# Low-rank and router product of tiles 1 to 3 as three rounded products of split operands

## The chip, the cores and the metric

The kernel runs on one core of one Trainium2 chip. The metric is the device time of one execution in microseconds (us), the median of three runs.

## What is computed

The input `x` holds 64 sequences of 32 tokens with 512 features. Two blocks are applied one after the other, each added to its input. Cut to what matters, the reference is:

```python
# block 0
base   = einsum('btd,od->bto', x, W)                  # W: 512 x 512
logits = einsum('btd,ed->bte', x, Wr) + 5.0 * one_hot(language)   # 8 experts
gates  = softmax over the two largest logits, 0 elsewhere
h      = einsum('btd,erd->bter', x, A)                # 8 experts x rank 16 = 128
x      = x + base + 2.0 * einsum('bter,bte,eor->bto', h, gates, B)
# block 1: an adapter of rank 16 per sequence, out of 64
x      = x + einsum('bnr,bor->bno', einsum('bni,bri->bnr', x, B1[id]), A1[id])
```

The two products in question here are `h` (128 columns) and the router's logits (8 columns). Both multiply `x`, so the kernel takes them as one product with 136 columns.

## The kernel before

The 2048 tokens are cut into four tiles (`NB` = 4) of `TB` = 512 tokens. Features lie on the 128 partitions in `K` = 4 blocks: `xs[:, t, k]` is block k of tile t, a 128 x 512 operand. Everything stays in SBUF. The code is written out by hand for each engine, with semaphores between the engines; each engine runs its list in order, so the order of the calls in the code is the order of the work.

**Operands.** A 32-bit operand can be used in two ways. A plain 32-bit operand (F32) goes into one `matmul` call, which the trace shows as two LDWEIGHTS and two MATMUL records. An operand of type float32r (F32R) has been rounded; a call with such operands shows one record of each. To keep the precision, the kernel splits an operand into a rounded part and a rounded rest (`x_hi` and `x_lo`, `w_hi` and `w_lo`, and so on) and takes three products: hi with hi, hi with lo, lo with hi. ScalarE makes the hi part (`round_hi`, L328), VectorE or GpSimd the rest (`split_lo`, L431; L309 on GpSimd for `x_lo` of tiles 1 to 3). `x_hi` and `x_lo` have two slots each, taken in turn by tile.

**TensorE's list per tile.** (`t` is the tile; names as in the code.)

- `base(t, c)`, L613, for output block c of four: 4 calls each on L631 (`w_hi` x `x_hi`), L637 (`w_lo` x `x_hi`) and L643 (`w_hi` x `x_lo`), all with 512 moving columns and accumulating in PSUM bank `main[c]`.
- `aw_first()` for tile 0 and `aw_tiles(u)` for tiles 1 to 3 (L675, L685): the product with 136 columns, in plain 32-bit form. The stationary operand is a 128 x 128 piece of `xs` (128 tokens), the moving one is `aws[:, k]`, 128 x 136. That is 4 token pieces x 4 blocks k = 16 calls (L673) per tile, into the two banks `aw_ps`. The last one signals `aw_done`.
- `gt_transposes(u)`, L696: four transposes of the gated `h`.
- `lora(t, c)`, L646: three products (L657 to L659) that add the low-rank output into `main[c]`.
- `down_part` (L725) and `up` (L749; `up_last`, L762 to L766, for the last tile): the two products of block 1.

The order is at L770 to L817. `aw_tiles(1)` stands between `lora(0, 0)` and `lora(0, 1)`; `aw_tiles(2)` and `aw_tiles(3)` stand behind the last `base` of the tile before and ahead of its `lora(t + 1, 3)`.

**The others.** VectorE waits on `aw_done`, forms the logits, their two largest and the gate (`top_two`, `pick`, `gate_h`), writes `gated`, and adds results to `xs` (L479 for block 0, L528 for block 1). ScalarE rounds `b0`, then takes the exponential of tile 0's gap (`exp_gap(0)`), then rounds `x` of tile 1 (L394 to L398). SyncE issues the loads and stores.

Of the kernel before, what the change touches and what calls it, by code (L numbers as in the profile page):

```python
# [39 lines left out]
P = 128  # L40
F32 = mybir.dt.float32
F32R = mybir.dt.float32r
# [11 lines left out]
def two_block_kernel(nc, x, adapter_id, adapter_list, language_id, w, aw, b0, a1, b1, out, *, tokens_per_batch,  # L54
# [22 lines left out]
    with ExitStack() as ctx:  # L77
        def sb(name, shape, dt=F32):
            return ctx.enter_context(nc.sbuf_tensor(name, shape, dt))
# [4 lines left out]
        def sem(name):  # L84
            return ctx.enter_context(nc.semaphore(name))
# [4 lines left out]
        ws = sb("ws", [P, K, K, P])  # L90
        w_hi, w_lo = sb("w_hi", [P, K, K, P], F32R), sb("w_lo", [P, K, K, P], F32R)
        aws = sb("aws", [P, K, AWN])
        b0s = sb("b0s", [P, D])
        b0_hi, b0_lo = sb("b0_hi", [P, D], F32R), sb("b0_lo", [P, D], F32R)
        rows = sb("rows", [P, SLOTS, D])
# [68 lines left out]
        exp_ready = sem("exp_ready")  # L164

        zeros_ready, w0_hi_ready, w0_lo_ready = sem("zeros_ready"), sem("w0_hi_ready"), sem("w0_lo_ready")
        b0_lo_ready = sem("b0_lo_ready")
        x0_lo_ready, x1_ready = sem("x0_lo_ready"), sem("x1_ready")
        gt_lo_ready = sem("gt_lo_ready")
        down_ready, down_lo_ready = sem("down_ready"), sem("down_lo_ready")  # L170
# [149 lines left out]
        @block.scalar  # L320
        def _(act):
            act.dma_start(aws[:, 0], aw[:, 0]).then_inc(aw_loaded[0], 16)
            act.dma_start(aws[:, 1:], aw[:, 1:]).then_inc(aw_loaded[1], 16)

            act.wait_ge(zeros_ready, 1)
            nc.scalar.activation(table_warm[:], zeros[:, 0:1], ACT.Exp)

            def round_hi(dst, src, ready):  # L328
                nc.scalar.activation(dst, src, ACT.Copy).then_inc(ready, 1)  # L329

            def w_half(c):
                act.wait_ge(w_loaded[c], 16)
                round_hi(w_hi[:, c], ws[:, c], w_hi_ready)

            def x_half(t, c):
                if t == 0:
                    act.wait_ge(x0_loaded[c], 16)
                elif c == 0:
                    act.wait_ge(x_loaded[t], 16)
                    if t >= 2:  # L340
                        act.wait_ge(base_done, (t - 1) * K)
                round_hi(x_hi[:, t % 2, c], xs[:, t, c], x_hi_ready)

            def a1_half(g):
                act.wait_ge(rows_loaded[g], 16)
                if g >= SLOTS:
                    act.wait_ge(up_done, PARTS * (g // GPB - 1))
                s = g % SLOTS
                if packed(g):
                    if g >= GPB:  # L350
                        act.wait_ge(a1_lo_ready, g - GPB + 1)
                    round_hi(a1_hi[:, g % GPB], rows[:, s], a1_hi_ready)
                else:
                    round_hi(a1_ops[:, s, 0], rows[:, s], a1_hi_ready)

            def pack_a1(g):

                act.wait_ge(a1_lo_ready, g + 1)
                s = g % SLOTS
                for h, own in enumerate(halves):  # L360
                    nc.scalar.activation(a1_ops[own, s, h], a1_hi[own, g % GPB], ACT.Copy)  # L361
                    last = nc.scalar.activation(a1_ops[halves[1 - h], s, h], a1_rest[own, g % GPB], ACT.Copy)  # L362
                last.then_inc(a1_packed, 1)

            def exp_gap(u):
                act.wait_ge(gap_ready, u + 1)
                nc.scalar.activation(gap_exp[:], gap[:], ACT.Exp).then_inc(exp_ready, 1)

            def gt_half(u):
                act.wait_ge(gt_done, u + 1)  # L370
                if u >= 1:
                    act.wait_ge(lora_done, u * K)
                round_hi(gt_hi[:], side[1][:], gt_hi_ready)

            def down_half(g):
                act.wait_ge(down_ready, g + 1)
                if g >= SLOTS:
                    act.wait_ge(up_done, PARTS * (g // GPB - 1))
                s = g % SLOTS
                if packed(g):  # L380

                    for to in (0, 1):
                        for h, own in enumerate(halves):
                            last = nc.scalar.activation(down_ops[halves[h ^ to], s, h, 0:GT // 2],  # L384
                                                        down[own, g % GPB, 0:GT // 2], ACT.Copy)
                        last.then_inc(down_hi_ready, 1)
                else:
                    round_hi(down_ops[:, s, 0], down[:, g % GPB], down_hi_ready)

            for c in range(K):  # L390
                x_half(0, c)
            for c in range(1, K):
                w_half(c)
            act.wait_ge(b0_loaded, 16)  # L394
            round_hi(b0_hi[:], b0s[:], b0_hi_ready)
            exp_gap(0)
            for c in range(K):
                x_half(1, c)  # L398
            gt_half(0)
            for t in range(NB - 1):  # L400
                if t == 0:
                    for g in range(GPB):
                        a1_half(g)
                    for g in range(GPB):
                        pack_a1(g)
                exp_gap(t + 1)
                for g in range(t * GPB, (t + 1) * GPB):
                    down_half(g)
                gt_half(t + 1)
                for g in range((t + 1) * GPB, (t + 2) * GPB):  # L410
                    a1_half(g)
                if t + 2 < NB:
                    for c in range(K):
                        x_half(t + 2, c)
                    for g in range((t + 1) * GPB, (t + 2) * GPB):
                        pack_a1(g)
            for g in range((NB - 1) * GPB, NG):
                down_half(g)
# [3 lines left out]
        def _(dve):  # L422
# [31 lines left out]
            def gate_h(u):  # L454

                dve.wait_ge(exp_ready, u + 1)
                then_wait(nc.vector.tensor_scalar(denom[:], gap_exp[:], 1.0, None, ALU.add))
                then_wait(nc.vector.reciprocal(inv[:], denom[:]))
                nc.vector.tensor_scalar(weight[:, :, 0], inv[:], SCALING0, None, ALU.mult)
                then_wait(nc.vector.scalar_tensor_tensor(weight[:, :, 1], gap_exp[:], SCALING0, inv[:],  # L460
                                                         ALU.mult, ALU.mult))

                then_wait(nc.vector.tensor_tensor(
                    picked_w[:], picked[:], weight[:].unsqueeze(3).broadcast_to([P, TILES, 2, experts]), ALU.mult))
                then_wait(nc.vector.tensor_tensor(gate[:], picked_w[:, :, 0], picked_w[:, :, 1], ALU.add))
                if u >= 1:
                    dve.wait_ge(gt_done, u)

                for j, h in h_parts(u):
                    last = nc.vector.tensor_tensor(  # L470
                        gated[:, j].rearrange("p j (e r) -> p j e r", e=experts),
                        h[:, :, 0:H].rearrange("p j (e r) -> p j e r", e=experts),
                        gate[:, j].unsqueeze(3).broadcast_to([P, j.stop - j.start, experts, rank]), ALU.mult)
                    if j.stop in (TILES // 2, TILES):
                        last.then_inc(gated_ready, 1)
# [96 lines left out]
            top_two(0)  # L572
            pick()
            gate_h(0)
            gt_rest(0)
            dve.wait_ge(const_ready, 4)
            then_wait(nc.vector.tensor_tensor(own_in_half[:], own_batch[:, 0:BPG // 2], own_batch[:, BPG // 2:],
# [34 lines left out]
        def _(pe):  # L612
# [54 lines left out]
            def lora_last(s):  # L667
                lora_products(K - 1, last_x1_banks[s][:, 0:GT], slice(s * GT, (s + 1) * GT))

            def aw_product(u, j, k):  # L670

                h = [h[:, j - js.start] for js, h in h_parts(u) if js.start <= j < js.stop][0]
                return nc.tensor.matmul(h, xs[:, u, k, j * P:(j + 1) * P], aws[:, k], start=(k == 0), stop=(k == K - 1))  # L673

            def aw_first():  # L675

                for k in range(K):
                    if k <= 1:
                        pe.wait_ge(aw_loaded[k], 16)
                    pe.wait_ge(x0_loaded[k], 16)  # L680
                    for j in range(TILES):
                        last = aw_product(0, j, k)
                last.then_inc(aw_done, 1)

            def aw_tiles(u):  # L685
                pe.wait_ge(x_loaded[u], 16)

                pe.wait_ge(gated_ready, u * 2)
                if u >= 2:
                    pe.wait_ge(x2_ready, (u - 1) * PARTS)  # L690
                for j in range(TILES):
                    for k in range(K):
                        last = aw_product(u, j, k)
                last.then_inc(aw_done, 1)

            def gt_transposes(u):  # L696
# [157 lines left out]
```

## Time and profile before

| what | value |
| --- | --- |
| median of 3 runs | 107.45 us |
| lowest and highest run | 106.88 and 107.86 us |
| profiled execution, span from first to last instruction | 104.8 us |
| mean granted TensorE clock over the span | 0.961 |
| TensorE busy (MATMUL records) | 93.5 us, 89% |
| TensorE weight loads | 78.2 us, 75% |
| VectorE, ScalarE, GpSimd busy | 68.0, 43.7, 39.0 us |

The profile is of one execution. It gives the span, from the first to the last instruction on the core; a run's time also holds what lies before and after, so the median lies 2.65 us above the span and the lowest run 2.1 us. In the profile, PE is TensorE's matmul side and PEld its weight loads; DVE is VectorE, ACT ScalarE, POOL GpSimd, SP SyncE. In names such as `aw_ps<-aws,xs` the output comes first, then the moving operand, then the stationary one; buffer numbers are left out (`b_hi` is `b0_hi`, `a_ops` is `a1_ops`). Both float32r and plain matmuls are printed as f32. A record's duration includes the time in the pipeline, so durations of neighbours overlap; the pace is read from start to start.

### The profile page before, as it was taken

The page shows a single profiled execution, that of the slowest core. Times are in us where ns is not written, and L with a number is a line of the kernel's source. Part 1 is how long each engine was busy: PE and PEld are TensorE (multiplying, and loading weights), DVE is VectorE, ACT ScalarE, POOL GpSimd, SP SyncE. Part 2 cuts the span into 40 slices and gives each one's busy share as a digit, 9 for nine tenths or more (in the row PEclk, how much of TensorE's full clock was granted, in tenths as well). Part 3 has the DMA queues.
Part 4 walks back from the last instruction along what each step waited for, and adds up shares of the span by engine and source line. Part 5 has one row for each costly group of instructions (what it writes and reads, how often), then busy time and mean ns, then how long its engine had stood idle before and what let it go on. Part 6 is the DMA issues. An engine that isn't in the chain of part 4 may idle for free.

```text
span 104.8 us, 2166 instructions
## 1 busy us (share of the span) xinstructions
PE 93.5 (89%) x733; PEld 78.2 (75%) x733; DVE 68.0 (65%) x220; ACT 43.7 (42%) x88; POOL 39.0 (37%) x42
## 2 busy tenths in 40 slices
PE   5999995009999999999999999999999999999970
PEld 2597882008799788988898888888988888898860
DVE  1269989994421997498604983988029839891890
ACT  3472604405693069802970489009803840000300
POOL 4002986996920000699900004998000072000000
PEclk9999999965599999999999999999999999999997
DMA  2999807426993693222569200222600002314046
GB/s 36 356 348 291 362 19 181 131 62 113 422 276 95 126 356 72 59 55 58 145 154 324 104 0 0 100 100 47 260 0 0 3 0 69 137 52 149 6 168 232
DMA packets 14989, 14.33 MB, mean 137 GB/s; under 512 B 10114, under 2 KB 11394, under 8 KB 14594
## 3 DMA queue, kind: packets, MB, share of 16 engines
q1 hardware_dynamic: 14050, 11.82, 35.1%
q0 software_dynamic: 640, 2.10, 7.2%
q10 hardware_dynamic: 288, 0.28, 1.1%
q8 instruction: 6, 0.10, 0.4%
q14 instruction: 5, 0.04, 0.1%
HBM read 9.99 MB, written 4.19 MB: 135 GB/s over the span
## 4 chain that ended last, share of the span: by engine, by line
PE 87%; issue 7%; DVE 3%; DVEq 0%
PE main L631 15%; PE main L637 14%; PE main L643 14%; PE aw_ps L673 12%; PE side L725 5%; PE main L658 3%; PE main L657 3%; PE main L659 3%; PE aw_ps L749 3%; PE main L772 3%; PE side L673 2%; DVE xs L520 2%; PE side L705 2%; PE main L749 1%; PE side L749 1%
## 5 line engine op out<-in xcount | busy, mean ns | idle before, releaser
L309 POOL TENSOR_TENSOR x_lo<-xs,x_hi 128x512 fp32r<-128x512 f32 x12 | 15.0, 1284 | 25.7 <-ACT x_hi L329 25.7
L631 PE MATMUL main<-x_hi,w_hi 128*128 128x512 f32 (+1 forms) x64 | 18.6, 414 | 0.0
L637 PE MATMUL main<-x_hi,w_lo 128*128 128x512 f32 (+1 forms) x64 | 17.7, 400 | 0.0
L643 PE MATMUL main<-x_lo,w_hi 128*128 128x512 f32 (+1 forms) x64 | 17.0, 387 | 0.0
L637 PEld LDWEIGHTS main<-x_hi,w_lo 128*128 128x128 f32 x64 | 12.4, 197 | 2.8
L673 PE MATMUL aw_ps<-aws,xs 128*128 128x136 f32 x112 | 14.1, 279 | 0.0
L643 PEld LDWEIGHTS main<-x_lo,w_hi 128*128 128x128 f32 x64 | 12.1, 192 | 2.6
L673 PEld LDWEIGHTS aw_ps<-aws,xs 128*128 128x128 f32 x112 | 13.7, 190 | 0.2
L631 PEld LDWEIGHTS main<-x_hi,w_hi 128*128 128x128 f32 x64 | 11.8, 197 | 2.5 <-DVE w_hi L543 0.2
L361 ACT ACTIVATE a_ops<-a_hi 64x512 fp32r<-64x512 f32 x12 | 7.6, 630 | 10.7 <-POOL a_rest L293 10.6
L479 DVE TENSOR_TENSOR xs<-main,xs 128x512 f32<-128x512 f32 x15 | 9.9, 683 | 2.8 <-PE main L659 2.8
L384 ACT ACTIVATE down_ops<-down 64x128 fp32r<-64x128 f32 x24 | 7.4, 309 | 6.3 <-DVE down L494 5.9
L329 ACT ACTIVATE x_hi<-xs 128x512 fp32r<-128x512 f32 x16 | 9.0, 619 | 1.7 <-DMA xs<-x_t 1.7
L528 DVE TENSOR_TENSOR xs<-aw_ps,xs 128x256 f32<-128x256 f32 x24 | 9.2, 415 | 0.1
L277 POOL DMA_INDIRECT rows<-a_t,row_at x8 | 8.7, 1087 | 1.5 <-issue 1.1
L438 DVE TENSOR_TENSOR logits<-aw_ps,bias 128x16 f32<-128x16 f32 (+1 forms) x8 | 1.0, 164 | 12.6 <-PE aw_ps L673 12.6
L705 PE MATMUL side<-ident,gated 128*128 128x128 f32 x16 | 2.9, 312 | 6.6 <-issue 6.6
L293 POOL TENSOR_TENSOR a_rest<-rows,a_hi 128x512 f32<-128x512 f32 x6 | 7.7, 1292 | 0.6 <-ACT a_hi L329 0.6
L528 DVE TENSOR_TENSOR xs<-main,xs 128x256 f32<-128x256 f32 x12 | 4.5, 419 | 5.2 <-PE main L749 5.1
L705 PEld LDWEIGHTS side<-ident,gated 128*128 128x128 f32 x16 | 2.1, 156 | 7.5 <-issue 7.0
L362 ACT ACTIVATE a_ops<-a_rest 64x512 fp32r<-64x512 f32 x12 | 7.6, 630 | 0.1
L293 POOL TENSOR_TENSOR a_ops<-rows,a_ops 128x512 fp32r<-128x512 f32 x2 | 2.5, 1292 | 11.6 <-ACT a_ops L329 11.6
(111 smaller groups left out, 145.8 us busy)
## 6 DMA issues: line engine op xcount, KB each, us to landing
out_t<-xs SPq DMA_DIRECT2D x16, 256.0 KB, 2.3
xs<-x_t SPq DMA_DIRECT2D x3, 1024.0 KB, 6.4
b1s<-b_t SPq DMA_DIRECT2D x64, 32.0 KB, 2.0
xs<-x_t SPq DMA_DIRECT2D x4, 256.0 KB, 4.2
ws<-w_t SPq DMA_DIRECT2D x4, 256.0 KB, 5.6
b0s<-b_t SPq DMA_DIRECT2D x1, 256.0 KB, 5.6
aws<-aw_t ACTq DMA_DIRECT2D x1, 204.0 KB, 4.0
rows<-a_t,row_at POOLq DMA_INDIRECT x8, 4.0
```

The source lines that it names most:

```text
L277: nc.gpsimd.indirect_dma_start(rows[:, g % SLOTS], None, a1, bass.IndirectOffsetOnAxis(ap=row_at[:, g:g + 1], axis=0)).then_inc(rows_loade ...
L293: nc.gpsimd.tensor_tensor(lo, rows[:, s], hi.bitcast(F32), ALU.subtract).then_inc(a1_lo_ready, 1)
L309: nc.gpsimd.tensor_tensor(x_lo[:, t % 2, c], xs[:, t, c], x_hi[:, t % 2, c].bitcast(F32), ALU.subtract).then_inc(x_lo_ready, 1)
L329: nc.scalar.activation(dst, src, ACT.Copy).then_inc(ready, 1)
L361: nc.scalar.activation(a1_ops[own, s, h], a1_hi[own, g % GPB], ACT.Copy)
L362: last = nc.scalar.activation(a1_ops[halves[1 - h], s, h], a1_rest[own, g % GPB], ACT.Copy)
L479: nc.vector.tensor_tensor(xs[:, t, c], main[c][:], xs[:, t, c], ALU.add).then_inc(x1_ready, 1)
L528: return nc.vector.tensor_tensor(to, up_banks[i][:].rearrange("p (h q n) -> p h q n", h=2, q=2)[:, :, part], to, ALU.add)
L631: nc.tensor.matmul(out_ap, w_hi[:, c, k], x_hi[:, s, k, n], start=(k == 0), stop=False)
L637: nc.tensor.matmul(out_ap, w_lo[:, c, k], x_hi[:, s, k, n], start=False, stop=False)
L643: last = nc.tensor.matmul(out_ap, w_hi[:, c, k], x_lo[:, s, k, n], start=False, stop=False)
L673: return nc.tensor.matmul(h, xs[:, u, k, j * P:(j + 1) * P], aws[:, k], start=(k == 0), stop=(k == K - 1))
```

## The change

Tiles 1 to 3 take the product with 136 columns as three products of split operands; tile 0 stays as it is. `aw_tiles` issues 48 calls per tile in place of 16, with the pieces of `x_hi` and `x_lo` that `base` uses as the stationary operand and `aw_hi` or `aw_lo` as the moving one. Two new tensors and two semaphores hold the split of `aws`. ScalarE makes `aw_hi` between `b0_hi` and `exp_gap(0)`; VectorE makes `aw_lo` between `gate_h(0)` and `gt_rest(0)`. `aw_tiles` now waits for `x_hi` and `x_lo` of its tile where it waited for the tile's load.

```diff
+        aw_hi, aw_lo = sb("aw_hi", [P, K, AWN], F32R), sb("aw_lo", [P, K, AWN], F32R)
...
             round_hi(b0_hi[:], b0s[:], b0_hi_ready)
+            act.wait_ge(aw_loaded[0], 16)
+            act.wait_ge(aw_loaded[1], 16)
+            round_hi(aw_hi[:], aws[:], aw_hi_ready)
             exp_gap(0)
...
             gate_h(0)
+            dve.wait_ge(aw_hi_ready, 1)
+            split_lo(aw_lo[:], aws[:], aw_hi[:], aw_lo_ready)
             gt_rest(0)
...
             def aw_tiles(u):
-                pe.wait_ge(x_loaded[u], 16)
+                s = u % 2
+                pe.wait_ge(x_hi_ready, (u + 1) * K)
+                pe.wait_ge(x_lo_ready, u * K)
+                if u == 1:
+                    pe.wait_ge(aw_hi_ready, 1)
+                    pe.wait_ge(aw_lo_ready, 1)
 
                 pe.wait_ge(gated_ready, u * 2)
                 if u >= 2:
                     pe.wait_ge(x2_ready, (u - 1) * PARTS)
                 for j in range(TILES):
+                    h, n = h_tile(u, j), slice(j * P, (j + 1) * P)
                     for k in range(K):
-                        last = aw_product(u, j, k)
+                        nc.tensor.matmul(h, x_hi[:, s, k, n], aw_hi[:, k], start=(k == 0), stop=False)
+                        nc.tensor.matmul(h, x_hi[:, s, k, n], aw_lo[:, k], start=False, stop=False)
+                        last = nc.tensor.matmul(h, x_lo[:, s, k, n], aw_hi[:, k], start=False, stop=(k == K - 1))
                 last.then_inc(aw_done, 1)
```

On TensorE, at the place of tile 1's product between `lora(0, 0)` and `lora(0, 1)`, the kernel before has this (a row is a line, an operation, output<-moving,stationary, the output's shape and a count):

```order
23 L657 MATMUL main<-gt_hi,b_hi 128x512
24 L658 MATMUL main<-gt_hi,b_lo 128x512
25 L659 MATMUL main<-gt_lo,b_hi 128x512
26 L673 MATMUL aw_ps<-aws,xs 128x136 x16
27 L657 MATMUL main<-gt_hi,b_hi 128x512
```

and the changed kernel has this (its lines are numbered a few higher; L663 to L665 are the products of `lora`). The three rows 26 to 28 come 16 times in a row, up to row 73:

```order
23 L663 MATMUL main<-gt_hi,b_hi 128x512
24 L664 MATMUL main<-gt_hi,b_lo 128x512
25 L665 MATMUL main<-gt_lo,b_hi 128x512
26 L704 MATMUL aw_ps<-aw_hi,x_hi 128x136
27 L705 MATMUL aw_ps<-aw_lo,x_hi 128x136
28 L706 MATMUL aw_ps<-aw_hi,x_lo 128x136
```

Sixteen calls have become 48 at the same place, and two of each three neighbours have the same stationary piece of `x_hi`. The other two tiles read alike.

On ScalarE, ahead of tile 0's exponential, the changed kernel has one row more (8):

```order
6 L330 ACTIVATE w_hi<-ws 128x512 x3
7 L330 ACTIVATE b_hi<-b0s 128x512
8 L330 ACTIVATE aw_hi<-aws 128x544
9 L368 ACTIVATE gap_exp<-gap 128x4
10 L330 ACTIVATE x_hi<-xs 128x512 x4
```

On VectorE, behind tile 0's gating, the changed kernel has one row more (31):

```order
30 L474 TENSOR_TENSOR gated<-aw_ps,gate 128x128 x2
31 L436 TENSOR_TENSOR aw_lo<-aws,aw_hi 128x544
32 L436 TENSOR_TENSOR gt_lo<-side,gt_hi 128x512
33 L583 TENSOR_TENSOR own_in_half<-own_batch 128x4
34 L483 TENSOR_TENSOR xs<-main,xs 128x512
```

Nothing else has moved on these two engines; the lists of GpSimd and SyncE are as before.

## Rows read from the trace of the kernel before

**Rows 1.** The page: span, busy time, and slices of TensorE and its clock.

```profile
span 104.8 us, 2166 instructions
...
PE 93.5 (89%) x733; PEld 78.2 (75%) x733; DVE 68.0 (65%) x220; ACT 43.7 (42%) x88; POOL 39.0 (37%) x42
...
PE   5999995009999999999999999999999999999970
...
PEclk9999999965599999999999999999999999999997
```

**Rows 2.** Who waited for whom on TensorE: us in total, times, longest.

```profile
PE side L705 <- issue: 6.6, 1, 6.6
PE main L772 <- DVE zeros L537: 1.3, 1, 1.3
```

**Rows 3.** The chain that ended last, in order: start us, us, what.

```profile
8.07 0.46 PE aw_ps L673 x4
8.54 0.04 issue
8.57 1.20 PE main L631 x4
...
17.05 6.56 issue
23.61 1.12 PE side L705 x4
24.73 1.71 PE main L631 x4
...
29.91 3.71 PE aw_ps L673 x32
...
39.94 0.44 PE side L705 x4
40.37 0.94 PE main L631 x4
...
52.66 3.71 PE aw_ps L673 x32
...
74.04 3.71 PE aw_ps L673 x32
...
93.17 0.48 PE main L637 x4
```

**Rows 4.** Timeline of TensorE, 96.85 to 97.45 us: matmul records of three float32r products.

```profile
96.86 0.39 PE L657 MATMUL aw_ps<-gt_hi,b_hi 128*128 128x256 f32 x1
97.09 0.28 PE L658 MATMUL aw_ps<-gt_hi,b_lo 128*128 128x256 f32 x1
97.21 0.28 PE L659 MATMUL aw_ps<-gt_lo,b_hi 128*128 128x256 f32 x1
```

**Rows 5.** The same timeline, weight loads.

```profile
96.86 0.19 PEld L657 LDWEIGHTS aw_ps<-gt_hi,b_hi 128*128 128x128 f32 x1
96.97 0.19 PEld L658 LDWEIGHTS aw_ps<-gt_hi,b_lo 128*128 128x128 f32 x1
```

**Rows 6.** Timelines of ScalarE and VectorE around the two new instructions.

```profile
12.27 0.61 ACT L329 ACTIVATE b_hi<-b0s 128x512 fp32r<-128x512 f32 x1
17.26 0.20 ACT L367 ACTIVATE gap_exp<-gap 128x4 f32<-128x4 f32 x1 [4.38 <-DVE gap L443]
...
23.48 0.48 DVE L470 TENSOR_TENSOR gated<-aw_ps,gate 128x128 f32<-128x128 f32 x2
25.40 0.69 DVE L432 TENSOR_TENSOR gt_lo<-side,gt_hi 128x512 fp32r<-128x512 f32 x1 [1.44 <-ACT gt_hi L329]
...
30.01 0.69 DVE L479 TENSOR_TENSOR xs<-main,xs 128x512 f32<-128x512 f32 x1 [2.75 <-PE main L659]
```

**Rows 7.** Timeline of GpSimd: the rests of x for tiles 1, 2 and 3.

```profile
18.07 4.92 POOL L309 TENSOR_TENSOR x_lo<-xs,x_hi 128x512 fp32r<-128x512 f32 x4 [0.92 <-ACT x_hi L329]
...
42.78 5.06 POOL L309 TENSOR_TENSOR x_lo<-xs,x_hi 128x512 fp32r<-128x512 f32 x4 [13.19 <-ACT x_hi L329]
...
64.20 5.06 POOL L309 TENSOR_TENSOR x_lo<-xs,x_hi 128x512 fp32r<-128x512 f32 x4 [11.55 <-ACT x_hi L329]
```

More of the change, by code:

```diff
@@ L166, in two_block_kernel @@
         zeros_ready, w0_hi_ready, w0_lo_ready = sem("zeros_ready"), sem("w0_hi_ready"), sem("w0_lo_ready")
-        b0_lo_ready = sem("b0_lo_ready")
+        b0_lo_ready, aw_hi_ready, aw_lo_ready = sem("b0_lo_ready"), sem("aw_hi_ready"), sem("aw_lo_ready")
         x0_lo_ready, x1_ready = sem("x0_lo_ready"), sem("x1_ready")
@@ L668, in lora_last, with h_tile @@
                 lora_products(K - 1, last_x1_banks[s][:, 0:GT], slice(s * GT, (s + 1) * GT))
-            def aw_product(u, j, k):
-                h = [h[:, j - js.start] for js, h in h_parts(u) if js.start <= j < js.stop][0]
-                return nc.tensor.matmul(h, xs[:, u, k, j * P:(j + 1) * P], aws[:, k], start=(k == 0), stop=(k == K - 1))
+            def h_tile(u, j):
+                return [h[:, j - js.start] for js, h in h_parts(u) if js.start <= j < js.stop][0]
             def aw_first():
@@ L681, in aw_first @@
                     for j in range(TILES):
-                        last = aw_product(0, j, k)
+                        last = nc.tensor.matmul(h_tile(0, j), xs[:, 0, k, j * P:(j + 1) * P], aws[:, k],
+                                                start=(k == 0), stop=(k == K - 1))
                 last.then_inc(aw_done, 1)
             def aw_tiles(u):
-                pe.wait_ge(x_loaded[u], 16)
+                s = u % 2
[4 more added lines that the diff above has]
+                    pe.wait_ge(aw_lo_ready, 1)
                 pe.wait_ge(gated_ready, u * 2)
```

## The prediction

> **What bounds the kernel now.** I read the page first. TensorE is busy for 93.5 of 104.8 us, and its line of slices stands at 9 from the tenth slice to the thirty-eighth of forty [rows 1]. The next question is whether it ever waits. The view of waits on TensorE names two waits in the whole span: 1.3 us ahead of the very first matmul and 6.6 us ahead of the transposes of tile 0 [rows 2]. The chain of work that ended last puts the second one at 17.05 to 23.61 us [rows 3]; from there TensorE's list runs through without a wait. So a microsecond more or less in TensorE's list after 23.6 us is a microsecond more or less in the time, unless the change makes some other engine late. The product with 136 columns of tiles 1 to 3 lies in this part: three stretches of 3.71 us, at 29.91, 52.66 and 74.04 us [rows 3], 11.1 us together.
>
> **What is removed.** Each stretch is 16 plain calls, shown as 32 pairs of a weight load and a matmul. 3.71 us by 32 is 0.116 us from one pair to the next, or 0.232 us a call. The clock is at 9 tenths or more in all slices of that part [rows 1], which is the 2.4 GHz level. 0.116 us at 2.4 GHz is 278 cycles, and twice 136 columns is 272: each record of the plain form streams its 136 columns twice and nothing else is seen. A plain call thus costs four passes of 136 columns.
>
> **What is added on TensorE.** 48 calls of the rounded form. A rounded call shows one pair of records. With 256 columns it takes 0.12 us (0.48 us for 4 [rows 3]); 256 columns at 2.4 GHz are 0.107 us, so it is one pass. One pass of 136 columns is 0.057 us, and 48 of them would be 2.7 us, which would be 1.0 us less per tile. That is what the change looks like on paper. But the stream is not the only thing in a pair.
>
> The other thing is the weight load: each call brings its own 128 x 128 stationary operand. As a rule it is hidden behind the stream of the call before. Its true length shows only where TensorE comes out of a gap. At 96.86 us it does. The load for L657 starts at 96.86 and that for L658 at 96.97, 0.11 us later [rows 5]. The first matmul record lasts 0.39 us where its like last 0.28 [rows 4], so 0.11 us passed before it could begin. Both say that a load of 128 columns in the rounded form takes 0.11 us. The second load starts when the first matmul can begin, so one load at a time goes on ahead of the running matmul. In the plain form with 136 columns the load (0.11) hides exactly under two passes (0.116); with 256 columns in the rounded form it hides under one pass. With 136 columns in the rounded form the pass is 0.057 us and no longer covers it: the load sets the pace.
>
> No row shows a rounded call with fewer than 256 columns, so its price is bounded. From below by the load alone, which is printed as 0.11: at least 0.105 us. From above by the rounded call with 256 columns, since fewer columns can't take longer in the same form: 0.12 us [rows 3, 4]. The end nearest to the case is the load, because the stream is now well under it; I take 0.112 us. Then 48 x 0.112 = 5.38 us replace 3.71 us: +1.67 us per tile, and for three tiles +5.0 us. The ends: 48 x 0.105 = 5.04 us gives +4.0 us in all; 48 x 0.12 = 5.76 us gives +6.2 us.
>
> **The two new instructions.** `aw_hi` is a rounding of 544 columns; one of 512 takes 0.61 us [rows 6], so about 0.65 us. ScalarE stands idle for 4.38 us after `b_hi` until tile 0's gap comes from VectorE at 17.26 us [rows 6]; the two loads of `aws` that it waits for have landed long before, since TensorE is through with tile 0's product, which uses them, at 8.57 us [rows 3]. Cost nothing; without that idle time it would delay the exponential, and with it the transposes that TensorE waits for. `aw_lo` is a subtraction of 544 columns, about 0.73 us by the 0.69 us of `gt_lo` [rows 6]. VectorE has 1.44 us idle between the gating and `gt_lo` [rows 6], and it stands behind the gating, so the transposes don't wait for it. GpSimd can hold VectorE up at that time, and even if it came 1 us late, `gt_lo` is followed by 2.75 us of idle time before 30.01 us [rows 6]. Cost nothing. If the cover were gone, `gt_lo` would be late and `lora(0, 0)`, just ahead of 29.91 us, would wait.
>
> **The new waits.** `aw_tiles` now needs the split x of its tile. The four rests are done at 22.99, 47.84 and 69.26 us (start plus length [rows 7]); TensorE comes to the stretches at 29.91, 52.66 and 74.04 us. The slack is 6.9, 4.8 and 4.8 us. For tiles 2 and 3 the split itself starts after work of TensorE that shifts along with the rest, so the slack stays. Behind the waiting TensorE instruction everything would queue, but it won't wait.
>
> **What waits for the stretch.** VectorE's gating of the tile starts at `aw_done` and must be ready for the transposes at 39.94 us [rows 3]. The list of TensorE between the end of the stretch and the transposes is the same as before, and VectorE starts from the same signal, so both shift together: neither a gain nor a loss.
>
> **The sum.** Against the profiled execution: 104.8 + 5.0 = 109.8 us of span. The median of the runs lies 2.65 us above that span, which the change leaves alone: 107.45 + 5.0 = 112.45, say 112.5 us. The case's own range by the bounds is 111.1 to 113.9 us with 0.3 us for the measurement.
>
> **Rivals.**
>
> A. *The load is not what paces a narrow pair.* If loads of neighbours overlapped, the pace would be the stream plus what the 256-column call has above its stream (0.118 - 0.107 = 0.011): 0.068 us, 48 of them 3.3 us, -0.45 us per tile, -1.3 us in all: 106.1 us. For it: load records last 0.19 us and start 0.12 us apart, so their records do overlap. Against it: the load that started out of a gap took 0.11 us before the next could start [rows 5]. The Trainium skill, page "TensorE: Matmul & The Clock Gate", section "Back-to-back issue gap", has a pace in between: about 81 ns per load and matmul pair at 128 columns. By that figure the sum would be 48 x 81 ns = 3.9 us, +0.2 us per tile and 108.0 us in all; no run here has shown such a pair in 32-bit form. Chance 0.08, half of it faster by over 1%.
>
> B. *A repeated stationary operand is not loaded again.* Of each three calls two share the piece of `x_hi`. If its second load fell away, 32 loads of 0.112 us would remain per tile, 3.58 us, with the 48 passes (2.7 us) beneath them: -0.13 us per tile, -0.4 us in all, 107.1 us; the change would not be slower. It decides from one place, the pair L704 and L705: a load there or none. Against it: every matmul record of the page has a load record (733 and 733 [rows 1]); but no two neighbours before share an operand, so the trace can't exclude it. Chance 0.08.
>
> C. *A rounded call with few columns falls back to the pace of the plain one.* All rounded calls in the trace have 256 or 512 columns, all narrower ones are plain. If a rounded call with 136 columns took the 0.232 us of a plain one, 48 would be 11.1 us, +7.4 us per tile, +22.3 us in all: 129.8 us. Against it: nothing in the rows with 256 and 512 columns shows a step, both are one pass. Chance 0.10.
>
> D. *The clock falls.* In the stretches the array would stream for only 0.057 of each 0.112 us. The granted clock was seen to fall once, after the idle 6.56 us: the ninth to eleventh slices show 6, 5, 5 [rows 1], the 1.2 GHz level, where four calls of L631 took 1.71 us instead of 0.94 [rows 3]. If it fell in each stretch, the loads would take twice as long. Five microseconds at half speed in each of three places cost about 2.5 us each, +7.5 us on top: 120 us. Against it: TensorE stays in use, the records leave no gap, and no row shows a fall without idleness. Chance 0.08.
>
> **How the numbers follow.** The forecast keeps 0.66. What a measurement of this kernel can tell from no change is about 1%, 106.4 to 108.5 us. Faster by over 1%: half of A, 0.04. Within 1%: the other half of A and B, 0.12. Slower by over 1%: the forecast, C and D, 0.84. The range from 107.0 to 114.5 us takes in the forecast with its bounds, B, and half of A; it leaves out C, nearly all of D and half of A, some 0.2.
>
> **What would show it.** In the changed profile the three stretches should last 5.1 to 5.8 us each with 48 pairs of records, start to start 0.105 to 0.12 us, with no idle time on TensorE ahead of them and the wait of 6.6 us ahead of the transposes unchanged. TensorE's load time should grow and its clock should stay at 9 outside the three slices named. I am wrong if the stretch is near 3.3 us (A), if L705 has fewer loads than matmuls (B), if it is near 11 us (C), if the clock line shows new digits under 9 (D), or if TensorE waits for `x_lo`, `aw_hi` or `aw_lo`.

## The result and the profile after

The changed kernel takes 111.56 us (median of 4 runs, 111.08 to 111.96) against 107.47 us for the kernel before in the same runs (4 runs, 106.88 to 107.86). The ratio is 1.044 with a 95% interval of 1.037 to 1.051: slower by 4.1 us. A ratio and its interval are taken over the fast runs alone (those up to 1.5% above the fastest of their kernel), so a ratio can differ from that of two medians, which are of all runs. The forecast was 112.5 us. The profiled execution took 111.08 us, with a span of 109.0 us, 4.2 us longer than the span of before [rows 1].

The page of the changed kernel, the rows that answer to [rows 1]:

```profile
span 109.0 us, 2268 instructions
...
PE 98.3 (90%) x781; PEld 83.6 (77%) x781; DVE 68.3 (63%) x221; ACT 44.3 (41%) x89; POOL 39.0 (36%) x42
...
PE   5999994039999999999999999999999999999980
...
PEclk9999999655999999999999999999999999999999
```

TensorE's matmuls went from 93.5 to 98.3 us and its loads from 78.2 to 83.6 us, each with 48 records more (3 x 48 in place of 3 x 32). VectorE, ScalarE and GpSimd moved by 0.6 us at most. The clock line has the same dip of three slices under 9, one slice earlier; this will matter below.

The waits of TensorE in the changed kernel, as in [rows 2]:

```profile
PE side L718 <- DVE gated L474: 6.1, 1, 6.1
PE main L785 <- DVE zeros L541: 1.3, 1, 1.3
```

No wait was added; the one ahead of the transposes is 0.4 us shorter (6.13 us, 6.56 before), because TensorE comes to it later, and ends at 23.60 us where it ended at 23.61. The new time lies inside TensorE's own work. The chain of the changed kernel around the transposes of tile 0 and the product of tile 2 (start us, us, what), against [rows 3]:

```profile
23.60 1.11 PE side L718 x4
24.72 1.71 PE main L637 x4
26.42 1.15 PE main L643 x4
27.58 0.93 PE main L649 x4
...
52.70 0.91 PE main L649 x4
53.61 0.06 PE aw_ps L704
53.67 0.11 PE aw_ps L705
53.78 0.11 PE aw_ps L706
53.90 0.11 PE aw_ps L704
...
58.92 0.28 PE main L663
59.21 0.23 PE main L664
```

The stretch runs from 53.61 to 58.92 us, and the first wide call behind it takes 0.28 us where its neighbour takes 0.23, since it waits 0.05 us for its own load. That is 5.31 + 0.05 = 5.36 us in place of 3.71 us: +1.65 us. The calls between 53.67 and 58.92 us are 47, which makes 0.1117 us each.

The two timelines of TensorE at the start of tile 1's stretch show what sets that pace. First the matmuls, then the weight loads:

```profile
29.04 0.23 PE L704 MATMUL aw_ps<-aw_hi,x_hi 128*128 128x136 f32 x1
29.11 0.28 PE L705 MATMUL aw_ps<-aw_lo,x_hi 128*128 128x136 f32 x1
29.22 0.27 PE L706 MATMUL aw_ps<-aw_hi,x_lo 128*128 128x136 f32 x1
...
29.05 0.19 PEld L705 LDWEIGHTS aw_ps<-aw_lo,x_hi 128*128 128x128 f32 x1
29.15 0.19 PEld L706 LDWEIGHTS aw_ps<-aw_hi,x_lo 128*128 128x128 f32 x1
29.27 0.19 PEld L704 LDWEIGHTS aw_ps<-aw_hi,x_hi 128*128 128x128 f32 x1
```

Every call has its load, L705 too, whose stationary operand is the one that L704 has just used. Each matmul of the stretch now starts some 0.06 us after its load's record, and the loads come 0.11 us apart, each some 0.05 us after the record of the running matmul. In the stretches of the kernel before, a load's record started right behind the running matmul's, mostly 0.001 to 0.002 us after it: there the stream was the longer part, and the pace was 0.1159 us.

### The profile page after: what moved, and what is told of

Read it like the earlier page. It is cut to its first block, busy times and chain, and to the rows that moved or that the text cites. A ratio compares the mean times of both kernels' runs of the same rounds, so it can differ in the third digit from the quotient of the medians.

```text
span 109.0 us, 2268 instructions
## 1 busy us (share of the span) xinstructions
PE 98.3 (90%) x781; PEld 83.6 (77%) x781; DVE 68.3 (63%) x221; ACT 44.3 (41%) x89; POOL 39.0 (36%) x42
## 4 chain that ended last, share of the span: by engine, by line
PE 73%; DVE 16%; DMA 5%; issue 1%; SPq 1%; ACT 1%; DVEq 0%
PE main L637 12%; PE main L643 11%; PE main L649 11%; PE side L738 5%; PE aw_ps L706 5%; PE aw_ps L705 5%; PE aw_ps L704 5%; DMA xs<-x_t 5%; PE main L663 3%; PE main L664 3%; PE main L665 3%; PE aw_ps L762 3%; DVE xs L524 2%; PE side L718 2%; PE main L762 1%
## 5 line engine op out<-in xcount | busy, mean ns | idle before, releaser
L643 PE MATMUL main<-x_hi,w_lo 128*128 128x512 f32 (+1 forms) x64 | 17.1, 390 | 0.0
L706 PE MATMUL aw_ps<-aw_hi,x_lo 128*128 128x136 f32 x48 | 13.2, 276 | 0.0
L705 PE MATMUL aw_ps<-aw_lo,x_hi 128*128 128x136 f32 x48 | 13.2, 274 | 0.0
L704 PE MATMUL aw_ps<-aw_hi,x_hi 128*128 128x136 f32 x48 | 13.0, 272 | 0.0
L704 PEld LDWEIGHTS aw_ps<-aw_hi,x_hi 128*128 128x128 f32 x48 | 9.2, 192 | 0.1
L705 PEld LDWEIGHTS aw_ps<-aw_lo,x_hi 128*128 128x128 f32 x48 | 9.2, 192 | 0.1
L706 PEld LDWEIGHTS aw_ps<-aw_hi,x_lo 128*128 128x128 f32 x48 | 9.2, 192 | 0.0
```

The costliest lines, as they stand in the source:

```text
L643: nc.tensor.matmul(out_ap, w_lo[:, c, k], x_hi[:, s, k, n], start=False, stop=False)
L704: nc.tensor.matmul(h, x_hi[:, s, k, n], aw_hi[:, k], start=(k == 0), stop=False)
L705: nc.tensor.matmul(h, x_hi[:, s, k, n], aw_lo[:, k], start=False, stop=False)
L706: last = nc.tensor.matmul(h, x_lo[:, s, k, n], aw_hi[:, k], start=False, stop=(k == K - 1))
```

## The experiments

Theory L: the loss is the load of a 32-bit stationary operand of 128 columns, 0.11 us, which one pass of 136 columns (0.057 us) no longer covers. Its rivals were: a narrow rounded call streams twice (S; 272 columns are 0.113 us, so the pace alone can't tell); any pair has a floor of 0.11 us (F); a part of the loss comes from the new instructions and waits. Ratios are to the kernel before in the same set of runs. Where only one run was made, it is read by its stretches and its span, not by its total. A stretch is the length of the product with 136 columns of one tile by the chain.

### The new instructions and waits without the 48 calls

```diff
                     for k in range(K):
-                        ... three calls with x_hi, x_lo, aw_hi, aw_lo ...
+                        last = nc.tensor.matmul(h, xs[:, u, k, n], aws[:, k], start=(k == 0), stop=(k == K - 1))
```

> The changed kernel with the plain 16 calls per tile back in place; the rounding of aws, its rest and the new waits stay. Theory L (the whole loss comes from the 48 weight loads): the time of before, 107.5 us within 1%, stretches of 3.71 us. Rival (a part of the loss comes from the new instructions or waits): over 108.5 us, with idle time on TensorE ahead of a stretch or a wait ahead of the transposes longer than 6.6 us.

Measured: 106.46 us (10 runs) against 106.63 us (13 runs), ratio 1.003, 0.998 to 1.009. In its chain the stretches are those of before, and the wait ahead of the transposes is still 6.6 us:

```profile
29.39 3.71 PE aw_ps L704 x32
...
52.12 3.71 PE aw_ps L704 x32
...
73.54 3.71 PE aw_ps L704 x32
```

The interval alone would leave room for 0.9 us; the chain shows no place for it, since no wait was added and the stretches are 3.71 us again. The loss is in the calls.

### 64 moving columns

```diff
-                        nc.tensor.matmul(h, x_hi[:, s, k, n], aw_hi[:, k], start=(k == 0), stop=False)
-                        ...
+                        for i, (a, b) in enumerate(((x_hi, aw_hi), (x_hi, aw_lo), (x_lo, aw_hi))):
+                            w = AWN if k == 0 and i == 0 else 64
+                            last = nc.tensor.matmul(h[:, 0:w], a[:, s, k, n], b[:, k, 0:w], ...
```

> Tiles 1 to 3 multiply only 64 of the 136 moving columns in 44 of the 48 calls (the other four per tile keep 136); the rest of the sum is left out. Theory L (a call costs the load of its 128 stationary columns): start to start stays at 0.112 us, stretches of 5.3 to 5.4 us, time as changed, about 111.5 us. Rival S (a narrow rounded call streams its columns twice, 272 columns being 0.113 us): 44 calls at 0.053 us, stretches of 2.8 us, about 104 us.

Measured: 117.27 us (one run, span 115.2 us), with about half of the changed kernel's columns. From the start of the first stretch to the end it took 85.2 us where the changed kernel took 79.8: 5.4 us more. The chain and the clock line of this run:

```profile
PEclk9999999855996799999985599999995899999998
...
30.01 5.28 PE aw_ps L706 x48
35.29 0.31 PE main L663
35.60 0.24 PE main L664
35.83 0.43 PE main L665
36.26 0.43 PE main L663
...
55.71 6.43 PE aw_ps L706 x48
```

Two things are to be read. The first stretch lasts 5.28 us, so the pace did not follow the columns: S is out, L and F stand. And behind the stretch the same wide calls take 0.43 us instead of 0.23, the 1.2 GHz level; the clock line has three new dips (slices 13 and 14, 21 to 23, 31 and 32). The first and the third begin within 0.6 us of the end of their stretch. The second begins inside its stretch, which takes 6.43 us for it: the granted clock is 1.00 from 55.5 to 59.5 us and 0.50 from 60 to 66 us. TensorE was not idle before any of them: the page has its busy line at 9 from slice 10 to slice 38. What it did before was 4 to 5.3 us of calls with 64 columns, each behind a full load. None of my theories had foreseen this for 64 columns; I had priced it as rival D for 136.

### 256 moving columns

```diff
-        aw_hi, aw_lo = sb("aw_hi", [P, K, AWN], F32R), sb("aw_lo", [P, K, AWN], F32R)
+        aw_hi, aw_lo = sb("aw_hi", [P, K, 256], F32R), sb("aw_lo", [P, K, 256], F32R)
```

with the added columns set to a constant and the output's pieces 256 columns apart.

> The moving operands of tiles 1 to 3 are padded from 136 to 256 columns; the padding's results are not used. Theory L: the stream of 256 columns (0.107 us) still lies under the load, the pace is that of the other rounded calls with 256 columns, 0.116 to 0.120 us, stretches of 5.6 to 5.8 us, 0.2 to 0.4 us more per tile, about 112.3 us. Rival S: twice 256 columns are 0.213 us, stretches of 10.2 us, about 126 us.

Measured: 113.58 us (one run, span 111.6 us). The chain ahead of and behind the second stretch:

```profile
54.43 0.91 PE main L652 x4
...
61.09 0.23 PE main L666
```

From 55.34 to 61.09 us the stretch is 5.75 us, 0.120 us a call: as L expected, and far from the 10.2 us of S. The total is 1.3 us over what I expected, and the stretches explain 1.2 us of the 2.6 us between this span and that of the changed kernel. The rest lies ahead of them: the 12 calls of `base(0, 3)` took 4.77 us here and 3.79 us there, and the transposes began 0.45 us later. The section on the hardware comes back to this.

### 64 stationary columns

```diff
+                            w = P if at == 0 else 64
+                            last = nc.tensor.matmul(h[0:w], a[:, s, k, j * P:j * P + w], b[:, k], ...
```

> In 44 of the 48 calls per tile only 64 of the 128 stationary columns (tokens) are loaded and multiplied, all 136 moving columns stay; the other half of the tokens is left out of those. Theory L: half a load is 0.054 us, now under the stream of 0.057 us, so start to start 0.06 to 0.07 us, stretches of 3.1 to 3.5 us, 1.9 to 2.3 us less per tile, about 105.2 us. Rival S, and rival F (a rounded pair has a floor of 0.11 us whatever its sizes): nothing changes, stretches of 5.36 us, 111.5 us.

Measured: 105.82 us (one run, span 103.9 us).

```profile
30.40 3.23 PE aw_ps L707 x48
```

Half the load, all 136 moving columns, and the stretch drops from 5.36 us to 3.23 + 0.05 = 3.28 us, with most starts 0.060 to 0.068 us apart. This is the run that decides between L and F: what the call costs is the number of stationary columns, until the stream takes over (the loads again start 0.002 to 0.004 us behind the running matmul). The narrower output isn't the cause: the bf16 run below reaches such a pace with all 128. Three stretches save 6.2 us, and the span is 5.1 us shorter than the changed kernel's; the rest went ahead of them, where the transposes began 0.6 us later and the 12 calls of `base(0, 3)` took 0.6 us longer.

### Two products instead of three

The line with `aw_lo` is left out, the other two stay.

> The product of x_hi with aw_lo is left out: 32 calls per tile in place of 48. Theory L: each call costs 0.112 us, so 16 fewer are 1.8 us less per tile, stretches of 3.5 to 3.6 us, 5.4 us less in all, about 106 us. Rival (the second of two calls with the same stationary x_hi was nearly free): stretches of 5 us and more, over 109 us.

Measured: 105.87 us (one run, span 103.9 us). The chain ahead of and behind the second stretch:

```profile
51.24 0.91 PE main L649 x4
...
55.67 0.28 PE main L663
```

From 52.15 to 55.67 us, 3.52 us, plus the 0.05 us of the wide call: 3.57 us for 32 calls, 0.112 us each. The omitted call had a stationary operand that was already in the array, and leaving it out saved as much as any other. A repeated operand is loaded again at full price.

### bf16 operands

```diff
+                        for i in range(3):
+                            last = nc.tensor.matmul(h, xb[:, k, n], awb[:, k], start=(k == 0 and i == 0), ...
```

> All 48 calls per tile of tiles 1 to 3 take bf16 operands (made once from tile 0 and from aws), so the results of these tiles are those of other data. ScalarE gets five roundings more in its idle time. Theory L: what costs is the load of a 32-bit stationary operand; the bf16 loads ahead of the first matmuls came 0.016 us apart, so the stream of 136 columns would set the pace, 0.057 to 0.07 us, stretches of 2.8 to 3.4 us, 2 to 2.5 us less per tile, about 104.5 us. Rival F (any load of 128 columns takes 0.11 us, whatever its type): stretches of 5.3 us, 111.5 us.

Measured: 104.67 us (one run, span 102.8 us).

```profile
30.36 2.86 PE aw_ps L709 x48
```

The same 48 calls with the same 136 columns take 2.86 us, 0.0596 us each: the stream of 136 columns (0.057 us) and 0.003 us. With bf16 the load of 128 columns is no longer seen. F is out a second time, and the price belongs to the 32-bit type. Both operands changed type here; that it is the stationary one's follows together with the run with 64 stationary columns. The Trainium skill, page "TensorE: Matmul & The Clock Gate", section "Weight-path perf modes — Fast Weight Load (FWL) and DoubleRow", says that the fast load is on for 128 weights when the input is not FP32; the two paces, 0.0596 and 0.1117 us, agree with it, if float32r counts as FP32 there.

### Wide calls set between the narrow ones

```diff
+                            if u == 1 and at % 5 == 4:
+                                ... one call of lora(0, 1 to 3), 512 columns, into main[c] ...
```

> The nine calls of tile 0's low-rank output for blocks 1 to 3 (512 columns, 0.23 us each) are set one by one behind every fifth of the first 45 narrow calls of tile 1, where before they followed all 48. Theory L with one load ahead: a wide call hides just the one load behind it, so the 57 calls last as long as apart, 5.36 + 2.10 = 7.4 to 7.5 us. Rival (loads can run two ahead): each wide call hides two loads, some 0.05 us less for each of nine, 7.0 us or less. The gates of tile 1 come 2 us later in the list of TensorE, so the transposes of tile 1 may wait for them; the total is not the measure here.

Measured: 112.89 us (one run, span 110.9 us). The chain inside the mixed stretch:

```profile
28.94 0.23 PE main L665
29.17 0.51 PE aw_ps L705 x5
29.68 0.28 PE main L711
...
36.28 0.30 PE aw_ps L705 x3
```

It runs from 29.17 to 36.58 us, 7.4 us for 57 calls. Apart, in the changed kernel, they take 5.36 + 9 x 0.234 = 7.47 us. Five narrow calls and a wide one take 0.51 + 0.28 = 0.79 us, which is 5 x 0.112 + 0.233: the wide call hides one load and no more. Had a second load gone ahead under it, 7.0 us would have been seen. The total is worse for what follows: the 64 calls of `down_part` end 3.2 us behind the stretch where the changed kernel needs 1.3 us, 1.1 us of it one wait for VectorE's additions.

### 100 moving columns

> As the run with 64 moving columns, with 100 of the 136 in 44 of 48 calls. There the pace stayed at 0.112 us, but the clock fell to half behind each of the three stretches. Theory L keeps the pace at 0.112 us here too, stretches of 5.3 us. [...]

The edit is that of the run with 64 columns, with 100. Measured: 111.65 us (one run, span 109.8 us).

```profile
PEclk9999999555699999999999999999999999999999
...
30.03 5.29 PE aw_ps L706 x48
```

The pace is again 0.11 us a call, and no dip follows the stretches, as with 136 columns. The slow part ahead of them is longer (four slices under 9); it explains why the span is 0.8 us above the changed kernel's.

### A version that beats both

The runs say what to cut: loads of 32-bit stationary operands. `x_hi` meets `aw_hi` and the router's rest in one call of 144 columns (16 calls), and the rest of x goes in as bf16 (16 calls). The product of `x_hi` with the rest of the 128 low-rank columns is left out.

```diff
+                    for k in range(K):
+                        nc.tensor.matmul(h, x_hi[:, s, k, n], aw_ops[:, k], start=(k == 0), stop=False)
+                    for k in range(K):
+                        last = nc.tensor.matmul(h[:, 0:AWN], x_lob[:, s, k, n], awb[:, k, 0:AWN], ...
```

> Aims under both kernels by cutting the loads of 32-bit operands from 48 to 16 per tile: x_hi meets 144 columns at once (aw_hi and the router's rest), and the rest of x is taken in bf16 with aws in bf16 (16 calls). Left out is the product of x_hi with the rest of the 128 low-rank columns. ScalarE makes the bf16 rest of x as GpSimd finishes it; VectorE adds two columns groups for the logits. Theory L: 16 x 0.112 + 16 x 0.059 = 2.7 us a stretch, 1.0 us less than the plain form, 2.9 us less in all than before (ratio 0.973), if the transposes don't wait for VectorE's added instruction (up to 0.3 us a tile). Rival F or a cost of changing between the two types: stretches of 3.5 us and more, no gain on before.

> The kernel with 16 rounded calls of 144 columns and 16 bf16 calls per tile once more, with more rounds, since its first ratio to before had no interval. Theory L: 0.973 to 0.985 of before; rival (its first lead was the moment at which the clock fell and rose): within 1% of before.

Measured: in the first set 105.40 us (4 runs) against 107.13 us (7 runs); in the second 105.04 us (6 runs) against 106.80 us (11 runs), ratio 0.971, 0.964 to 0.979. That ratio rests on two of the six runs of this kernel; the ratio of the medians of all runs is 0.984 in both sets. The first stretch in the chain of the second set's run:

```profile
30.51 0.40 PE aw_ps L718 x4
30.91 0.25 PE aw_ps L720 x4
31.17 0.45 PE aw_ps L718 x4
31.62 0.25 PE aw_ps L720 x4
...
33.29 0.29 PE main L677
```

Four rounded calls take 0.45 us, four bf16 ones 0.25 us; the stretch is 2.8 us, 0.9 us under the plain form. The change of type between groups costs next to nothing (16 x 0.1117 + 16 x 0.0596 = 2.74 us). TensorE waits 0.4 us in all for VectorE's additions, in two places; the second version below has VectorE's added instruction too and none of these waits, so that instruction alone isn't the cause. By the stretches and these waits some 2.2 us are gained, a ratio of 0.98. So the gain is clear, and its size lies nearer to 0.98 than to 0.971.

The second version uses the bf16 calls for the router's 8 columns only, so both rests are missing from the low-rank columns.

> As the last one, with the bf16 calls for the router's 8 columns alone; left out are both products with a rest for the 128 low-rank columns. Theory L: 16 x 0.112 us and 16 narrow calls of 0.03 us, stretches of 2.2 to 2.4 us, 4 us less than before in all (ratio 0.96). [...]

> The kernel with bf16 calls for the router's columns alone once more, with more rounds. Theory L: 0.96 to 0.975 of before; rival: within 1% of the kernel of the other run.

Measured: 103.15 us (6 runs) against 107.13 us; then 103.53 us (6 runs) against 106.80 us, ratio 0.967, 0.962 to 0.973. Its four calls of 8 columns take 0.10 us, the stretch 2.3 us:

```profile
30.36 0.40 PE aw_ps L718 x4
30.77 0.10 PE aw_ps L720 x4
...
32.68 0.33 PE main L677
```

Both versions buy time with precision: they leave out products with a rest, so the low-rank columns are less exact, by how much wasn't measured. With all three products in float32r nothing here beat the plain call.

## Why the prediction was right

**What bounds the kernel.** Right: TensorE's list runs through from the transposes on, before and after, and its added time is the added time of the whole. The run with the parts alone (ratio 1.003) and the halved load (3.23 us a stretch) show both directions. The wait ahead of the transposes was forecast unchanged at 6.6 us and measured 6.1 us, without effect on its end.

**The plain call's price.** Right: 3.71 us for 16 calls returned unchanged in the run with the new parts and the old calls. That it is two passes and not the load that sets 0.116 us per pair is a closer call than the prediction makes it, since a load of 0.112 us is almost as long; the place of the load records in the trace of before, right behind the running matmul's, speaks for the passes. No run varied the columns of a plain call.

**The added calls.** Right, and the size too: I took 0.112 us from the gap-side load of [rows 5] and it measured 0.1117 us; +1.67 us per tile forecast, +1.65 us measured. The upper bound, the rounded call with 256 columns, was measured in this place as 0.120 us. The step that mattered was to price a call not by its stream but by the load of the next one, which is only seen where TensorE comes out of a gap.

**The new instructions and waits.** Right: `aw_hi` went into ScalarE's idle time and `aw_lo` into VectorE's, the waits never held TensorE.

**The sum.** 3 x 1.65 = 4.95 us were added, but the span grew by 4.2 us. The missing 0.7 us is most likely no gain of the change, since it lies ahead of the first changed call. The 12 calls of `base(0, 3)` behind the transposes took 1.71 + 1.15 + 0.93 = 3.79 us after; before, they took 4.49 us, of which [rows 3] show the first four:

```profile
26.44 1.71 PE main L637 x4
28.14 1.07 PE main L643 x4
```

The granted clock tells why. From 26 to 28 us it was 0.50 before and 0.80 after (the column ahead of the last two):

```profile
26.00:28.00 2.00, 2.00 (x7) 1.52 (x6) 1.26 (x2) 1.12 (x3) 2.00 (x2) 0.50 1.00 414
...
26.00:28.00 2.00, 2.00 (x8) 1.60 (x8) 1.25 (x2) 1.11 (x3) 2.00 (x2) 0.80 1.01 414
```

It came back at 28.3 us before and at 26.8 us after, 1.5 us sooner, and half of that is the time won. What the sum had wrong is "104.8 + 5.0 = 109.8 us of span": it let one execution's slow part stand for both, and the span is 0.8 us shorter. The 2.65 us between span and median, called left alone, were 2.56 us. Together they are the 0.9 us between 112.5 and 111.56 us.

**The rivals.** A (the load doesn't pace a narrow pair, 106.1 us) fell with the pace of 0.1117 us and with the halved load. The Trainium skill's 81 ns per pair (page "TensorE: Matmul & The Clock Gate", section "Back-to-back issue gap") fit neither the rounded pairs (0.112 us) nor the bf16 ones (0.060 us), both with 136 columns. B (a repeated operand isn't loaded again) fell with the loads of L705 in the timeline and with the run with two products. C (0.232 us a call) fell with the pace. D (the clock falls) did not happen at 136 columns: the slice with a new digit under 9 belongs to the old dip, which came one slice earlier. But it is real: at 64 columns it cost about 5.4 us. I had given it 0.08 and the reason that no row showed a fall without idleness; one execution now shows three. Its reading of [rows 1] was loose too: the clock fell inside the idle time, not after it (granted 1.00 from 20 to 21 us, 0.75 from 21 to 22 us).

## What to carry to other kernels

A matmul with float32r operands costs the longer of its own stream and the load of the next stationary operand, here 0.112 us for 128 columns; where the stream was the longer one, it took 0.008 to 0.017 us more than its columns at 2.4 GHz (0.065 us for 136, 0.120 us for 256, 0.23 us for 512). Before splitting a plain product into three rounded ones, compare both with the plain call. Three rounded calls cost 0.335 us with 64, 100 and 136 columns alike, the plain call 0.232 us at 136. If the plain call's price grows with its columns, which no run shows, the two meet near 200 columns; that is an estimate from these two prices. Look for the bare load where TensorE comes out of a gap, since elsewhere the stream hides it. If narrow calls can't be avoided, take as many operands as precision allows in bf16, put all moving columns that share a stationary operand into one call, and look at the clock behind the stretch, not only at its pace.

## What the runs showed of the hardware that was not expected

The granted clock can fall to half behind work without a gap. During or behind stretches of 5.3 us of calls with 64 moving columns, each behind a full 32-bit load, it went to the 1.2 GHz level for several microseconds, three times in one execution, and from the first stretch on the kernel took 5.4 us longer than with 136 columns. Fewer columns made it slower. It didn't happen with 100 columns, nor with bf16 operands; each of these is one execution, and the cause isn't shown.

The slow part behind the idle time ahead of tile 0's transposes is not the same from one execution to the next. The same 12 calls of `base(0, 3)` took 3.6 us (two products), 3.7 us (parts alone), 3.8 us (changed), 4.5 us (before), 4.8 us (256 columns) and 5.1 us (100 columns and the first version with bf16, in its second set). That is 1.5 us of difference with nothing changed in them, and single runs of this kernel shouldn't be compared closer than that; by stretches, they can be compared to a few hundredths of a microsecond.
